# A hybrid of recurrent layers, FP4 feed-forward and attention: one root chain for both norms, the decay in PSUM, a product on GpSimd, and a new tick order

## The chip, the cores and the metric

The kernel runs on one core of a Trainium2 chip. The metric is device time in microseconds (us), the median over several executions. Of the core's engines, PE (TensorE) multiplies matrices, DVE (VectorE), ACT (ScalarE) and POOL (GpSimd) work element by element, and SP (SyncE) issues the DMAs. In this kernel all of POOL's operands lie in SBUF.

## What is computed

The input x is 16 sequences of 512 tokens with 128 channels, float32. In turn:

```
x = x + recurrent(layernorm(x))   # initial layernorm, then 4 layers
x = x + ffn(layernorm(x))         # 128 -> 352 -> 128, gated by silu, all operands through FP4 blocks of 16
x = x + attention(layernorm(x))   # causal, inner width 64
x = x + ffn(layernorm(x))         # the same weights
```

One recurrent layer is

```
h = layernorm(x); xk, xv, xr = mixes of h and h shifted by one token
k, v = xk @ Wk, xv @ Wv; sr = sigmoid(xr @ Wr)
# over tokens, with decay w and bonus u, kept in range by a running maximum pp:
out = (e1 * aa + e2 * v) / (e1 * bb + e2)     # aa, bb: decayed sums of weighted v and of weights
x = x + (sr * out) @ Wo
h = layernorm(x); x = x + sigmoid(mix_r @ Wcr) * (square(relu(mix_k @ Wck)) @ Wcv)
```

## The kernel before

All 16 sequences stay in SBUF (X, 128 partitions of tokens x 512). The work on one sequence in one layer is a job r, 64 of them (4 layers of 16); its channels x tokens tiles are 128 x 512. Each engine runs one Python loop over 133 **ticks**; in tick t the engine's order, written out by hand, calls step functions with a job number such as t - 5, and a function whose job doesn't exist does nothing. So a job goes through its steps over some 14 ticks, and many jobs are under way at once. Semaphores count finished steps; `Waits` drops waits that an engine has already passed. No planner runs: an engine executes its list in order, and a step that waits holds back what stands behind it.

Ticks 0 to 17 also normalise the input (`init_stats`, `init_rsqrt`, `init_z`, `init_affine`). `FFN_AT = NR + 3 = 67` is the base tick of 16 FFN jobs, 16 ticks later come 16 attention jobs, and 16 later 16 FFN jobs more; their steps (`mul_up`, `fh_*`, `fx_*`, `a_*`) stand in the same lists.

The steps that the text speaks of, with the tick offset of a job in the recurrent phase:
- A norm: `bn_stats` on DVE (L214), then on POOL a chain of four operations on 128 x 4 values (L590 to L595, with a pow to -1/2 at L593), each of them waiting for the one before where it uses it, then four ACT instructions (`normalise`, L734). Before, `rs1` (t - 2) and `rs2` (t - 8) run the chain once for each of the two norms of a layer.
- `turn1` transposes into PSUM bank T, `keep_h1` (ACT) takes it out; `sub_dh1` (POOL) and `mix_t`, `mix_rt` (DVE, L291, L298) mix h with its shift. `keys` (PE) writes bank K, `scan_pp` (L307) and `sub_d` read it. `args` and `exp_d` (ACT, L792 to L798) make decay and weight in the two halves of ed in SBUF; `arg_r`, `exp_r` make er.
- `mul_rv`, `mul_s1` multiply er and the weight with v (bank V, L328, L334; `mul_s1` writes back into bank V). `scan_bb` (L340) and `scan_aa` (L347) scan with the decay. `add_num` and `add_den` (POOL, L637, L631) add.
- `seeds` (ACT, L809) makes a first reciprocal rc of the denominator er, `mul_y` (DVE, L354) puts er * rc into bank K, `square_1` (ACT) squares, `mul_u`, `gated`, `scaled_p` (POOL), `rwkv` (L374) finish a cubic correction and the product with the gate; `output` (PE) and `add_xa` (L380) add to X.
- `turn2`, `keep_h2`, `sub_dh` (POOL, L650), `mix_k` (L391), `mix_r` (L398), `ff_keys` (L1090), `relu`, `square`, `ff_gate`, `tanh_c`, `ff_values` (L1107), `gate` and `add_xb` (POOL, L655) are the layer's second half.
- In the FFN jobs `fx_max`, `fh_max` take block maxima, `fx_scale` and `fh_scale` (DVE, `block_scale`, L243) the scales of 32 and 88 blocks, and POOL multiplies and divides by them (L671 to L690).

A PSUM bank has one owner at a time: `hand_over` returns the last use that a new owner must wait for. `lend_K` and `lend_O` hand a bank to a step of another engine.

## Time and profile before

| | us |
|---|---|
| median of three runs | 1459.57 (1458.12 to 1460.35) |
| the profiled execution | 1460.59 |
| its span, first to last instruction | 1459.0 |

| engine | busy us | share |
|---|---|---|
| PE | 1323.6 | 91% |
| DVE | 1344.3 | 92% |
| ACT | 1251.8 | 86% |
| POOL | 1248.4 | 86% |

The trace is of one execution. A busy share is an average over stages with different limits, so the rows below go by stretches of the span: the recurrent ticks fill it up to about 900 us, then come the first FFN, attention and the second FFN. In a timeline, times count from the span's start, and a bracket at the end of a row, where there is one, gives the idle time before it and what ended it. A duration contains what the instruction waits for inside itself.

### The profile page before, as it was taken

What the parts mean: (1) busy time and instruction counts of PE and PEld (TensorE: products, weight loads), DVE (VectorE), ACT (ScalarE), POOL (GpSimd) and SP (SyncE); (2) the same over time, 40 slices, a digit from 0 to 9 for tenths busy, and PEclk for the clock granted to TensorE, in tenths of its full rate; (3) what the DMA queues carried; (4) which work ended last, traced back from release to release, by engine and by line L of the source; (5) the groups of instructions that cost most, each with busy time, mean ns of one, the idle gap of its engine ahead of it and who ended that gap; (6) DMA issues with size and microseconds to landing.
All of it is one profiled execution on the core that took longest, in us unless ns stands there. A gap on an engine that the chain in (4) does not pass through costs nothing.

```text
span 1459.0 us, 23620 instructions
## 1 busy us (share of the span) xinstructions
PE 1323.6 (91%) x7245; PEld 936.5 (64%) x7245; DVE 1344.3 (92%) x2249; ACT 1251.8 (86%) x2459; POOL 1248.4 (86%) x1395
## 2 busy tenths in 40 slices
PE   3568899999999999999998999899999999989896
PEld 1235566666666666666666666676666788766675
DVE  6999999999999999999999999669999665799994
ACT  6679899999999999999988999778777888867764
POOL 6889999999999999999999999879998633388874
PEclk9679999999999999999999999999999999999999
DMA  7000000000000000000000000010000000000001
GB/s 222 0 1 1 1 1 1 1 1 31 2 1 1 1 1 1 1 2 1 1 1 1 1 1 8 22 30 23 23 1 2 1 1 1 1 8 24 28 22 37
DMA packets 26925, 18.56 MB, mean 13 GB/s; under 512 B 1072, under 2 KB 26160, under 8 KB 26800
## 3 DMA queue, kind: packets, MB, share of 16 engines
q1 hardware_dynamic: 26800, 17.05, 4.0%
q8 instruction: 59, 0.97, 0.3%
q14 instruction: 66, 0.54, 0.1%
HBM read 12.85 MB, written 4.19 MB: 12 GB/s over the span
## 4 chain that ended last, share of the span: by engine, by line
POOL 40%; DVE 22%; PE 18%; issue 14%; ACT 5%; POOLq 0%; DMA 0%; DVEq 0%; SPq 0%; ACTq 0%
POOL ln_rs L593 9%; POOL ln_rs L595 6%; POOL X L655 4%; POOL rv L637 4%; POOL ln_rs L590 3%; POOL dh L625 3%; POOL dh L650 3%; POOL ln_rs L591 3%; POOL er L631 3%; DVE hsc L240 3%; DVE W L450 3%; PE ps L1216 2%; PE ps L1198 2%; PE ps L1107 2%; DVE W L480 2%
## 5 line engine op out<-in xcount | busy, mean ns | idle before, releaser
L1107 PEld LDWEIGHTS ps<-W,kf 128*128 128x128 f32 x2048 | 245.2, 193 | 33.4 <-issue 28.6
L1090 PE MATMUL ps<-xk,W 128*128 128x512 f32 x512 | 255.7, 601 | 0.7 <-ACT er L874 0.7
L1107 PE MATMUL ps<-W,kf 128*128 128x128 f32 x2048 | 251.2, 276 | 1.1 <-DVE W L480 1.1
L734 ACT ACTIVATE z<-X,ln_rs 128x128 f32<-128x128 f32 x512 | 210.2, 487 | 4.7 <-POOL ln_rs L595 4.7
L593 POOL TENSOR_TENSOR ln_rs<-ln_rs,mhalf 128x4 f32<-128x4 f32 x128 | 174.0, 1360 | 0.0
L1007 PE MATMUL ps<-idn,z 128*128 128x128 f32 x664 | 105.6, 283 | 59.2 <-ACT h L828 36.7
L1007 PEld LDWEIGHTS ps<-idn,z 128*128 128x128 f32 x664 | 79.2, 144 | 122.4 <-issue 71.4
L835 ACT ACTIVATE kf<-ps 128x512 f32<-128x512 f32 x256 | 143.3, 585 | 5.5 <-PE ps L1090 5.5
L842 ACT ACTIVATE kf<-kf 128x1024 f32<-128x1024 f32 x128 | 134.3, 1049 | 0.0
L1090 PEld LDWEIGHTS ps<-xk,W 128*128 128x128 f32 x512 | 88.3, 193 | 62.1 <-issue 54.4
L1145 PE MATMUL ps<-WU,d 128*128 128x352 f32 x256 | 103.2, 485 | 20.9 <-DVE W L450 9.8
L690 POOL TENSOR_TENSOR W<-W,hsc 128x704 f32<-128x704 f32 x64 | 88.7, 1386 | 37.5 <-DVE W L480 37.5
L595 POOL TENSOR_TENSOR ln_rs<-ln_rs 128x4 f32<-128x4 f32 x128 | 107.2, 838 | 10.0
L874 ACT ACTIVATE er<-ps 128x352 f32<-128x352 f32 x128 | 58.7, 461 | 46.0 <-DVE W L450 31.5
L1138 PE MATMUL ps<-WG,d 128*128 128x352 f32 x256 | 97.5, 463 | 0.0
L214 DVE BATCH_NORM_STATS2 ln_st<-X 128x6 f32<-128x256 f32 x256 | 96.6, 418 | 0.2
L1046 PE MATMUL ps<-xt,W 128*128 128x512 f32 x128 | 73.0, 655 | 24.3 <-DVE rc L374 21.9
L1077 PEld LDWEIGHTS ps<-W,rc 128*128 128x128 f32 x512 | 71.6, 203 | 33.8 <-issue 33.8
L684 POOL TENSOR_TENSOR W<-W,hsc 128x704 f32<-128x704 f32 x64 | 88.4, 1394 | 2.9 <-DVE hsc L468 2.9
L631 POOL TENSOR_TENSOR er<-er,bb 128x512 f32<-128x512 f32 x64 | 84.9, 1326 | 4.2 <-DVE bb L340 3.5
L637 POOL TENSOR_TENSOR rv<-rv,aa 128x512 f32<-128x512 f32 x64 | 82.3, 1286 | 2.8 <-DVE aa L347 2.8
L809 ACT ACTIVATE rc<-er,seed 128x512 f32<-128x512 int32 x64 | 46.2, 722 | 44.3 <-POOL er L631 44.3
(167 smaller groups left out, 3987.9 us busy)
## 6 DMA issues: line engine op xcount, KB each, us to landing
X<-x_in SPq DMA_DIRECT2D x16, 256.0 KB, 6.8
xi<-x_in SPq DMA_DIRECT2D x16, 256.0 KB, 2.9
out<-X SPq DMA_DIRECT2D x16, 256.0 KB, 2.3
W<-weights SPq DMA_DIRECT2D x4, 832.0 KB, 8.5
W<-fp4w SPq DMA_DIRECT2D x1, 560.0 KB, 3.7
row<-rows SPq DMA_DIRECT2D x1, 192.0 KB, 3.1
wqkv<-qkv SPq DMA_DIRECT2D x1, 96.0 KB, 5.9
idn<-ident SPq DMA_DIRECT2D x1, 64.0 KB, 3.2
```

The costliest lines, as they stand in the source:

```text
L593: e.tensor_tensor(rs[:, 0, :], rs[:, 2, :], mhalf[:, :], ALU.pow).then_inc(*own.next())
L595: e.tensor_tensor(rs[:, 1, :], rs[:, 1, :], rs[:, 0, :], ALU.mult).then_inc(g.nr, 1)
L631: e.tensor_tensor(er[r % 2][:, :], er[r % 2][:, :], bb[r % 2][:, 0:T], ALU.add).then_inc(den_done, 1)
L637: e.tensor_tensor(rv[r % 2][:, :], rv[r % 2][:, :], aa[r % 2][:, 0:T], ALU.add).then_inc(num_done, 1)
L734: last = e.activation(chunk(dst, j), chunk(src, j), ACT.Identity, bias=rs[:, 1, j:j + 1], scale=rs[:, 0, j:j + 1])
L835: e.activation(kf[r % 3][:, f, :], (pF0, pF1)[f % 2][:, :], ACT.Relu).then_inc(relu_done[f], 1)
L842: e.activation(both, both, ACT.Square).then_inc(sq_done[k], 1)
L1007: last = e.transpose(chunk(dst, j), chunk(src, j), idn[:, :])
L1090: e.matmul((pF0, pF1)[f % 2][:, :], w_of(r, WCK + f), xk[r % 2][:, :], start=True, stop=True).then_inc(kf_mm[f], 1)
L1107: last = e.matmul(chunk(pKV, j), kf[r % 3][:, f, j * 128:(j + 1) * 128], w_of(r, WCV + f), start=f == 0 and j == 0, stop=f == 3, skip_grou ...
L1138: e.matmul(pG[j % 2][:, 0:I], chunk(fx[n % 2], j), WG[:, :], start=True, stop=True).then_inc(g_mm, 1)
L1145: e.matmul(pU[j % 2][:, 0:I], chunk(fx[n % 2], j), WU[:, :], start=True, stop=True).then_inc(u_mm, 1)
```

## The change

- `Norm` objects of the two norms share their buffers: one chain, `rsqrts(s)`, works on 128 x 8 values, the first norm of job s beside the second norm of job s - 6. It runs once a tick.
- `exp_d` is split. `exp_k` writes the weight in SBUF, `exp_d` writes the decay into bank T, lent by `lend_T` after `keep_h1` and taken back by `turn2` when `scan_aa` is done. `lend_K` goes.
- `mul_s1` writes weighted v to a new SBUF tile s1. Bank V is free for the next job when `mul_s1` is done.
- `mul_y` moves from DVE to POOL and multiplies in place in er; `square_1` and `rwkv` read er in SBUF.
- FFN_AT is NR + 4, so there are 134 ticks. The order of each engine's steps is new, and several steps run one tick later. The recurrent steps in their new order (offset from t; before in the printed lists):
  - DVE: `mix_t` 5, `mix_k` 10, `gated` 7, `mix_r` 11, `mul_rv` 6, `add_xa` 8, `mul_s1` 6, `scan_bb` 6, `scan_aa` 6, `bn2` 8, `scan_pp` 5, `bn1` 2, `sub_d` 5, `mul_u` 7, `gate` 13, `rwkv` 7, `mix_rt` 4, `arg_r` 5.
  - POOL: `scaled_p` 7, `mul_y` 7, `sub_dh1` 4, `add_xb` 14, `add_num` 6, `add_den` 6, `sub_dh` 9, `rsqrts` 2.
  - ACT: `exp_k` 6, `relu` 0, `exp_r` 6, `keep_h1` 4, `tanh_c` 13, `exp_d` 6, `relu` 1, `square` 1 of job 13, `norm2` 9, `relu` 2, `norm1` 3, `square_1` 7, `keep_h2` 9, `tanh_r` 6, `relu` 3, `square` 0 of job 12, `args` 5, `seeds` 6.
  - PE: `ff_keys` 0, `ff_gate` 13, `turn1` 4, `values` 6, `ff_keys` 1, `output` 8, `lend_T` 6, `ff_keys` 2, `receptance` 6, `ff_values` 0 of job 13, `keys` 5, `ff_keys` 3, `turn2` 9, `ff_values` 1.
  - FFN steps, DVE: `fh_add` 0, `fx_max`, `fh_sub` 0, `mul_up` 3, `fx_scale`, `fh_max`, `fh_add` 1, `fh_scale`, `fh_sub` 1, the two inverses, `fx_add`, `mul_up` 0, `fx_sub`, `mul_up` 1, `mul_up` 2, `f_bn`. POOL: `f_rsqrt`, `fh_scaled` 0, `add_res`, `fh_scaled` 1, `fh_divided` 0, `fx_scaled`, `fh_divided` 1, `fx_divided`.
- Two waits are new at the FFN's start: `silu` waits for the last `rwkv`, `keep_hq` for the last `scan_bb`.

```diff
@@ -29,7 +29,8 @@
 KC = [(0, 128), (128, 128), (256, 96)]
 
 Q_AT = 55
-FFN_AT = NR + 3
+FFN_AT = NR + 4
+LN2_LAG = 6
...
 
         class Norm:
-            def __init__(self, name, size):
-                self.size = size
-                self.stats, self.nr, self.z = [sem(f"{name}_{k}") for k in ("stats", "nr", "z")]
-                self.st = ring(name + "_st", size, [128, NT, 3])
-                self.rs = ring(name + "_rs", size, [128, 3, NT])
+
+            def __init__(self, name, size, lag=0, beside=None):
+                self.size, self.lag = size, lag
+                self.stats, self.z = sem(name + "_stats"), sem(name + "_z")
+                if beside:
+                    self.nr, self.st2, self.rs2, at = beside.nr, beside.st2, beside.rs2, NT
+                else:
+                    self.nr, at = sem(name + "_nr"), 0
+                    self.st2, self.rs2 = ring(name + "_st", size, [128, 2 * NT, 3]), ring(name + "_rs", size, [128, 3, 2 * NT])
+                self.st, self.rs = [k[:, at:at + NT, :] for k in self.st2], [k[:, :, at:at + NT] for k in self.rs2]
+                self.of = lambda r, n: r[(n + lag) % size]
...
-        rv, rc, ag = [ring(k, 2, [128, T]) for k in ("rv", "rc", "ag")]
+        s1, rv, rc, ag = [ring(k, 2, [128, T]) for k in ("s1", "rv", "rc", "ag")]
...
+        n_2 = Norm("ln2", 3, LN2_LAG, n_1)
...
-                w.wait_ge(g.nr, n - g.size + 1)
+                w.wait_ge(g.nr, n + g.lag - g.size + 1)
                 for k in range(NT // 2):
-                    last = e.bn_stats(g.st[n % g.size][:, 2 * k:2 * k + 2, :].rearrange("p a s -> p (a s)"),
+                    last = e.bn_stats(g.of(g.st, n)[:, 2 * k:2 * k + 2, :].rearrange("p a s -> p (a s)"),
                                       src[:, k * 256:(k + 1) * 256].rearrange("p (a c) -> p c a", a=2))
...
             def arg_r(r):
                 if 0 <= r < NR:
-                    w.wait_ge(y_done, r - 1)
+                    w.wait_ge(rwkv_done, r - 1)
                     w.wait_ge(d_done, r + 1)
...
             def mul_s1(r):
                 if 0 <= r < NR:
+                    w.wait_ge(ek_done, r + 1)
+                    w.wait_ge(v_mm, r + 1)
+                    w.wait_ge(aa_done, r - 1)
+                    e.tensor_tensor(s1[r % 2][:, :], ed[r % 2][:, 1, :], pV[:, :], ALU.mult).then_inc(s1_done, 1)
+
+            def scan_bb(r):
+                if 0 <= r < NR:
+                    w.wait_ge(den_done, r - 1)
+                    w.wait_ge(ek_done, r + 1)
                     w.wait_ge(ed_done, r + 1)
-                    w.wait_ge(rv_done, r + 1)
-                    e.tensor_tensor(pV[:, :], ed[r % 2][:, 1, :], pV[:, :], ALU.mult).then_inc(s1_done, 1)
-
-            def scan_bb(r):
-                if 0 <= r < NR:
-                    w.wait_ge(den_done, r - 1)
+                    e.tensor_tensor_scan(bb[r % 2][:, 1:T + 1], pT[:, :], ed[r % 2][:, 1, :], 0.0,
+                                         ALU.mult, ALU.add).then_inc(bb_done, 1)
+
+            def scan_aa(r):
+                if 0 <= r < NR:
+                    w.wait_ge(num_done, r - 1)
                     w.wait_ge(ed_done, r + 1)
-                    e.tensor_tensor_scan(bb[r % 2][:, 1:T + 1], ed[r % 2][:, 0, :], ed[r % 2][:, 1, :], 0.0,
-                                         ALU.mult, ALU.add).then_inc(bb_done, 1)
-
-            def scan_aa(r):
-                if 0 <= r < NR:
-                    w.wait_ge(num_done, r - 1)
                     w.wait_ge(s1_done, r + 1)
-                    e.tensor_tensor_scan(aa[r % 2][:, 1:T + 1], ed[r % 2][:, 0, :], pV[:, :], 0.0,
+                    e.tensor_tensor_scan(aa[r % 2][:, 1:T + 1], pT[:, :], s1[r % 2][:, :], 0.0,
                                          ALU.mult, ALU.add).then_inc(aa_done, 1)
-
-            def mul_y(r):
-                if 0 <= r < NR:
-                    w.wait_ge(*lent_K[r])
-                    w.wait_ge(seed_done, r + 1)
-                    e.tensor_tensor(pK[:, :], er[r % 2][:, :], rc[r % 2][:, :], ALU.mult).then_inc(y_done, 1)
...
             def rwkv(r):
                 if 0 <= r < NR:
                     w.wait_ge(u_done, r + 1)
-                    e.scalar_tensor_tensor(out=rc[r % 2][:, :], in0=pK[:, :], scalar=2.0, in1=p[r % 2][:, :],
+                    e.scalar_tensor_tensor(out=rc[r % 2][:, :], in0=er[r % 2][:, :], scalar=2.0, in1=p[r % 2][:, :],
...
-            def rsqrt(g, n, scale=1.0, eps=EPS):
-                rs, st = g.rs[n % g.size], g.st[n % g.size]
+            def roots(rs, st, done, scale=1.0, eps=EPS):
+                k = st.shape[1]
                 w.wait_ge(consts, PADS)
-                w.wait_ge(g.z, n - g.size + 1)
-                w.wait_ge(g.stats, n + 1)
                 e.tensor_scalar(rs[:, 2, :], st[:, :, 2], scale / 128.0, eps, ALU.mult, ALU.add).then_inc(*own.next())
                 e.tensor_scalar(rs[:, 1, :], st[:, :, 1], -1.0, None, ALU.mult)
                 w.wait_ge(*own.so_far())
-                e.tensor_tensor(rs[:, 0, :], rs[:, 2, :], mhalf[:, :], ALU.pow).then_inc(*own.next())
+                e.tensor_tensor(rs[:, 0, :], rs[:, 2, :], mhalf[:, 0:k], ALU.pow).then_inc(*own.next())
                 w.wait_ge(*own.so_far())
-                e.tensor_tensor(rs[:, 1, :], rs[:, 1, :], rs[:, 0, :], ALU.mult).then_inc(g.nr, 1)
+                e.tensor_tensor(rs[:, 1, :], rs[:, 1, :], rs[:, 0, :], ALU.mult).then_inc(done, 1)
+
+            def rsqrt(g, n, scale=1.0, eps=EPS):
+                w.wait_ge(g.z, n - g.size + 1)
+                w.wait_ge(g.stats, n + 1)
+                roots(g.of(g.rs, n), g.of(g.st, n), g.nr, scale, eps)
...
-            def rs1(r):
-                if 0 <= r < NR:
-                    rsqrt(n_1, r)
-
-            def rs2(r):
-                if 0 <= r < NR:
-                    rsqrt(n_2, r)
+            def rsqrts(s):
+
+                if 0 <= s < NR + LN2_LAG:
+                    lo, hi = 0 if s < NR else NT, 2 * NT if s >= LN2_LAG else NT
+                    w.wait_ge(n_1.z, min(s - 2, NR))
+                    w.wait_ge(n_2.z, s - LN2_LAG - 2)
+                    w.wait_ge(n_1.stats, min(s + 1, NR))
+                    w.wait_ge(n_2.stats, s - LN2_LAG + 1)
+                    roots(n_1.rs2[s % 3][:, :, lo:hi], n_1.st2[s % 3][:, lo:hi, :], n_1.nr)
...
+            def mul_y(r):
+                if 0 <= r < NR:
+                    w.wait_ge(seed_done, r + 1)
+                    e.tensor_tensor(er[r % 2][:, :], er[r % 2][:, :], rc[r % 2][:, :], ALU.mult).then_inc(y_done, 1)
...
             def exp_d(r):
                 if 0 <= r < NR:
+                    w.wait_ge(*lent_T[r])
                     w.wait_ge(args_done, r + 1)
-                    e.activation(ed[r % 2][:, :, :], ed[r % 2][:, :, :], ACT.Exp, scale=-1.0).then_inc(ed_done, 1)
+                    e.activation(pT[:, :], ed[r % 2][:, 0, :], ACT.Exp, scale=-1.0).then_inc(ed_done, 1)
+
+            def exp_k(r):
+                if 0 <= r < NR:
+                    w.wait_ge(args_done, r + 1)
+                    e.activation(ed[r % 2][:, 1, :], ed[r % 2][:, 1, :], ACT.Exp, scale=-1.0).then_inc(ek_done, 1)
...
-                    e.activation(pO[:, :], pK[:, :], ACT.Square, bias=seed[:, 1:2]).then_inc(sq1_done, 1)
+                    e.activation(pO[:, :], er[r % 2][:, :], ACT.Square, bias=seed[:, 1:2]).then_inc(sq1_done, 1)
...
             def values(r):
                 if 0 <= r < NR:
-                    w.wait_ge(*bV.hand_over(aa_done, r + 1))
+                    w.wait_ge(*bV.hand_over(s1_done, r + 1))
...
-            def lend_K(r):
-
-                if 0 <= r < NR:
-                    lent_K[r] = bK.hand_over(rwkv_done, r + 1)
+            def lend_T(r):
+
+                if 0 <= r < NR:
+                    lent_T[r] = bT.hand_over(aa_done, r + 1)
```

## Rows read from the trace of the kernel before

**Rows 1.** Windows: start:end length, busy (count) of PE, PEld, DVE, ACT, POOL, clock, DMA.

```profile
208.60:691.60 483.00, 466.29 (x2522) 322.25 (x2521) 483.00 (x736) 461.47 (x841) 466.07 (x491) 1.00 0.01 3
889.60:1009.20 119.60, 113.44 (x637) 83.20 (x636) 93.26 (x158) 97.70 (x187) 103.77 (x113) 0.97 0.08 23
1009.20:1072.20 63.00, 59.95 (x340) 42.72 (x339) 63.00 (x109) 50.56 (x103) 61.55 (x67) 1.00 0.06 18
1175.60:1229.80 54.20, 54.20 (x366) 43.98 (x365) 33.30 (x105) 46.09 (x134) 20.27 (x35) 1.00 0.00 1
1309.80:1397.90 88.10, 79.67 (x454) 57.97 (x453) 88.10 (x143) 67.14 (x137) 72.10 (x78) 1.00 0.09 25
```

**Rows 2.** DVE timeline: start us, duration us, engine, line, operation, out<-in.

```profile
499.51 0.66 DVE L380 TENSOR_TENSOR X<-X,ps 128x512 f32<-128x512 f32 x1
...
501.37 1.42 DVE L398 SCALAR_TENSOR_TENSOR xc<-dh,vec,h 128x512 f32<-128x512 f32 x1
...
503.37 0.69 DVE L354 TENSOR_TENSOR ps<-er,rc 128x512 f32<-128x512 f32 x1
...
505.04 0.74 DVE L391 SCALAR_TENSOR_TENSOR xk<-dh,vec,h 128x512 f32<-128x512 f32 x1
505.70 1.21 DVE L340 TENSOR_TENSOR_SCAN bb<-ed 128x512 f32<-128x512 f32 x1
...
507.42 0.68 DVE L360 SCALAR_TENSOR_TENSOR p<-ps,p 128x512 f32<-128x512 f32 x1
...
513.31 0.65 DVE L380 TENSOR_TENSOR X<-X,ps 128x512 f32<-128x512 f32 x1
```

**Rows 3.** POOL timeline of the same tick.

```profile
500.97 1.27 POOL L637 TENSOR_TENSOR rv<-rv,aa 128x512 f32<-128x512 f32 x1
...
505.23 1.67 POOL L595 TENSOR_TENSOR ln_rs<-ln_rs 128x4 f32<-128x4 f32 x1
506.99 0.56 POOL L590 TENSOR_SCALAR ln_rs<-ln_st 128x4 f32<-128x4 f32 x1
...
507.82 1.04 POOL L593 TENSOR_TENSOR ln_rs<-ln_rs,mhalf 128x4 f32<-128x4 f32 x1
...
509.09 1.27 POOL L631 TENSOR_TENSOR er<-er,bb 128x512 f32<-128x512 f32 x1
510.32 1.03 POOL L650 TENSOR_TENSOR dh<-h 128x512 f32<-128x512 f32 x1
```

**Rows 4.** FFN: POOL timeline; then L243's instructions, ns min/median/max.

```profile
1050.88 0.19 POOL L590 TENSOR_SCALAR ff_rs<-ff_st 128x4 f32<-128x4 f32 x1
...
1052.62 1.39 POOL L690 TENSOR_TENSOR W<-W,hsc 128x704 f32<-128x704 f32 x1
...
L243 DVE TENSOR_SCALAR xsc<-xsc x32: 160/492/1234, 936.1 to 1404.3; 128x32 f32<-128x32 f32 x32
L243 DVE TENSOR_SCALAR hsc<-hsc x32: 195/522/1393, 973.7 to 1438.6; 128x88 f32<-128x88 f32 x32
```

**Rows 5.** Waits, 208.6 to 691.6 us, ACT and PE: total, times, longest.

```profile
ACT rc L809 <- POOL er L631: 21.5, 35, 0.6
...
PE ps L1007 <- ACT h L828: 16.7, 35, 0.5
```

**Rows 6.** Groups by line: count, busy us, mean ns, idle before.

```profile
L798 ACT ACTIVATE ed<-ed 128x1024 f32<-128x1024 f32 x64 | 68.0, 1063 | 0.0
...
L803 ACT ACTIVATE er<-er 128x512 f32<-128x512 f32 x64 | 40.8, 638 | 1.4 <-DVE er L321 1.4
```

**Rows 7.** PE timeline of a recurrent tick.

```profile
507.77 1.88 PE L1090 MATMUL ps<-xk,W 128*128 128x512 f32 x4
509.49 1.02 PE L1046 MATMUL ps<-xt,W 128*128 128x512 f32 x2
...
512.96 1.95 PE L1107 MATMUL ps<-W,kf 128*128 128x128 f32 x16
```

**Rows 8.** Line 307's instructions: ns min/median/max, first and last start.

```profile
L307 DVE TENSOR_TENSOR_SCAN pp<-wneg,ps x64: 1182/1193/1244, 26.4 to 902.3; 128x512 f32<-128x512 f32 x64
```

More of the change, by code:

```diff
@@ L519, in vector @@
             for t in range(TICKS):
-                fh_max(ffn_job(t - 7))
+                mix_t(t - 5)
+                fh_add(ffn_job(t - 8), 0)
+                fx_max(ffn_job(t - 3))
+                a_mask(att_job(t - 7), 3)
+                fh_sub(ffn_job(t - 8), 0)
+                init_affine(t - 2)
+                mul_up(ffn_job(t - 7), 3)
+                fx_scale(ffn_job(t - 3))
+                fh_max(ffn_job(t - 7))
+                weights_rounded(t - Q_AT - 6)
+                mix_k(t - 10)
@@ L521, in vector @@
+                gated(t - 7)
+                mix_r(t - 11)
+                mul_rv(t - 6)
+                a_max(att_job(t - 7), 3)
+                add_xa(t - 8)
+                mul_s1(t - 6)
+                scan_bb(t - 6)
+                prepare(t - 3)
                 fh_add(ffn_job(t - 8), 1)
+                scan_aa(t - 6)
                 fh_scale(ffn_job(t - 7))
+                a_inverse(att_job(t - 8))
                 fh_sub(ffn_job(t - 8), 1)
-                mul_up(ffn_job(t - 6), 0)
@@ L525, in vector @@
[L525 to L533 removed]
+                fx_inverse(ffn_job(t - 3))
+                fh_inverse(ffn_job(t - 7))
+                a_add(att_job(t - 8))
+                bn2(t - 8)
@@ L543, in vector @@
-                a_max(att_job(t - 6), 1)
-                mul_y(t - 7)
-                mix_t(t - 4)
-                arg_r(t - 5)
-                a_mask(att_job(t - 6), 2)
-                a_max(att_job(t - 6), 2)
-                mix_k(t - 10)
-                init_affine(t - 1)
-                scan_bb(t - 6)
-                gated(t - 6)
-                weights_scales(t - Q_AT)
-                mul_u(t - 7)
-                mul_rv(t - 5)
-                rwkv(t - 7)
-                gate(t - 12)
@@ L954, in scalar @@
             for t in range(TICKS):
+                keep_hq(ffn_job(t - 9), 0)
+                silu(ffn_job(t - 7), 3)
+                put_x(ffn_job(t - 9))
+                keep_hq(ffn_job(t - 9), 2)
+                exp_k(t - 6)
+                keep_hq(ffn_job(t - 9), 1)
+                relu(t - 11, 0)
+                exp_r(t - 6)
+                keep_h1(t - 4)
+                tanh_c(t - 13)
+                fh_magic(ffn_job(t - 8), 1)
+                exp_d(t - 6)
+                relu(t - 11, 1)
@@ new lines, in tensor @@
+                ff_gate(t - 13)
+                turn1(t - 4)
+                values(t - 6)
+                lend_M(ffn_job(t - 8), 1)
+                ff_keys(t - 11, 1)
+                output(t - 8)
+                lend_T(t - 6)
+                f_turn(ffn_job(t - 5))
+                ff_keys(t - 11, 2)
+                f_gate(ffn_job(t - 6), 0)
+                p_values(att_job(t - 8))
+                receptance(t - 6)
+                down(ffn_job(t - 9))
+                f_up(ffn_job(t - 6), 0)
@@ new lines, in tensor @@
+                p_turn(att_job(t - 7), 0)
+                lend_X(ffn_job(t - 4))
+                f_gate(ffn_job(t - 6), 1)
+                f_up(ffn_job(t - 6), 1)
+                ff_values(t - 13, 0)
+                similarity(att_job(t - 6), 0)
+                p_turn(att_job(t - 7), 1)
+                keys(t - 5)
+                f_gate(ffn_job(t - 6), 2)
+                lend_O(t - 7)
+                similarity(att_job(t - 6), 1)
+                ff_keys(t - 11, 3)
+                turn2(t - 9)
```

204 lines of the change are left out of this document (79 added, 125 removed).

## The prediction

> **What bounds the kernel now.** The busy shares of the whole span are close together on four engines, so no share alone names the bound. The table by stretch [rows 1] gives four stages. From 208.6 to 691.6 us (35 recurrent ticks) the span per tick is 483.0/35 = 13.80 us; DVE is busy all of it, PE 96.5%, ACT 95.5%, POOL 96.5%. From 1009.2 to 1072.2 (6 ticks of the first FFN) a tick is 10.5 us, with DVE full and POOL 61.55 of 63. From 1309.8 to 1397.9 (8 ticks of the second) it is 11.0, DVE full, POOL only 72.1 of 88.1. From 1175.6 to 1229.8 (7 ticks of attention) it is 7.74, and PE is busy 54.2 of 54.2: PE bound, and the change takes nothing off PE.
>
> The DVE's timeline of one recurrent tick [rows 2] shows what "full" means. `add_xa` returns after 513.31 - 499.51 = 13.80. An instruction starts about 0.08 before its predecessor's recorded end (505.04 + 0.74 against 505.70), so an operation's place is its duration less 0.08. `mix_r` takes 1.42 where `mix_k`, the same form, takes 0.74: 0.68 is a wait inside the instruction. So DVE's own work is 13.12 a tick. POOL's timeline [rows 3] shows for what. GpSimd is in `add_num` until 502.24 when `mix_r` starts at 501.37; and POOL's first chain of tiny operations (L590 to L595) takes until 506.99, so 4.75 us, the second 509.09 - 506.99 = 2.10. The same chain in the FFN takes 1052.62 - 1050.88 = 1.74 [rows 4]. The slow stretch is exactly where DVE runs operations with two SBUF inputs or in a double-rate form, back to back from `mix_r` (501.37) to `mul_u` (507.42): 6.05 us, 5.37 without the wait. L595 starts at 505.23 and ends at 506.90, when `scan_bb` (505.70 + 1.21) ends. These DVE operations and POOL's exclude each other.
>
> That gives a sum for POOL. Big operations: four at 1.23 (510.32 - 509.09) and two at 0.99 (1.03 less the same 0.04) are 6.90. Two chains less their pow of 1.04, which mostly runs while DVE holds its inputs, are 2 x (1.74 - 1.04) = 1.40. DVE's excluding stretch is 5.37. Together 13.67, against 13.80 measured; 0.13 is loss at the seams. **So DVE and POOL together bound the tick.** ACT has 0.61 idle a tick (21.5/35, behind the denominator on POOL) and PE 0.48 (16.7/35, behind h2) [rows 5]: ACT has 13.19 of work, PE 13.32 with its pipeline drain, about 13.15 without.
>
> Were the exclusion strict for the pow too, the tick before would be 6.90 + 2 x 1.74 + 5.37 = 15.75; the trace has 13.80, so the pow is not held out for its whole length.
>
> The Trainium skill ("SBUF — State Buffer", section "Who interferes with whom") calls this an exclusive lock between a DVE operation with two SBUF inputs and a GpSimd one that reads SBUF: the later one blocks until the other ends. It speaks against moving one more SBUF operation to GpSimd, and taken at its word for the pow as well it gives the second rival's time, where the trace only half agrees.
>
> **The change, part by part (recurrent tick).**
> - `mul_y` leaves DVE: -0.61 (0.69 less 0.08) there, and +1.23 on POOL, priced by `add_den` [rows 2, 3].
> - One chain for both norms: POOL loses a chain of 1.74. The pow gets eight columns for four. No row has one of eight: it costs between 1.04 (all fixed) and 2.08 (all per column). I take 2.08, since the chain's three other operations share 0.70 with their gaps, which leaves most of a pow looking like work per column; but it hides under DVE's excluding stretch either way.
> - Decay in PSUM: `scan_bb` now has one SBUF input and leaves the excluding stretch (-1.13 there, no change on DVE's own time; between 0 and 0.05 for reading PSUM, I take 0). `rwkv` now reads er and p from SBUF and enters it (+0.66, the place of `mix_k`; +0.06 on DVE). Weighted v in SBUF: at nothing, its inputs are one SBUF and one PSUM as before; bank V comes free earlier.
> - The double-width exp (L798, 1.063) becomes two of 512 columns (L803, 0.638 each) [rows 6]. Less one start overlap of 0.11 that is +0.11 on ACT. `square_1` reads SBUF: this exp, SBUF to SBUF, is the nearest row, and a price between 0 and 0.05 is left; I take 0.
> - New order: `rwkv`, `mix_rt`, `arg_r`, `mix_t`, `mix_k`, `gated`, `mix_r` follow each other round the tick's end. The excluding stretch is 5.37 - 0.61 - 1.13 + 0.66 = 4.29, and POOL's chain is issued last in its tick, opposite it.
>
> New sums. DVE: 13.12 - 0.61 + 0.06 = 12.57. POOL with the stretch: 6.90 + 1.23 + 0.70 + 4.29 = 13.12, plus the same seam loss 13.25. ACT: 13.30. PE: 13.15 to 13.32. Four limits within 0.75, so the tick can't fall to DVE's 12.57. Do the waits fit? On PE a 512-column product takes 2 x 0.43 = 0.86 (four instructions in 509.49 - 507.77 = 1.72) and one half of the FFN values 1.8, so 0.9 for eight and 0.45 for four small products [rows 7]. In the new order, from `ff_keys` 0 on, `turn1` is done at 0.86 + 0.9 + 0.45 = 2.2, and `turn2` starts at 2.2 + 1.72 (values) + 0.86 + 0.9 + 0.86 + 0.86 + 1.8 + 0.86 + 0.86 = 10.9. Keys of the recurrent part are done at 10.0, so DVE's `scan_pp` starts there, and by DVE's order (0.68 for `bn2`, 1.13 for each scan) `scan_aa` ends at 9.4: bank T's new loan to the decay keeps about 1.4 of slack; if it didn't, `turn2` would wait with the second half of the FFN values behind it on PE, and `keep_h2` behind that on ACT. On DVE `scan_bb` now waits for the separate decay exp, with `scan_aa`, `bn2` and `scan_pp` behind it; the exp follows `turn1` (2.2), h1, and a tanh, so it ends by about 6, and the scan is due at 7.1. Estimates from the same rows: the denominator's product on POOL is done near 8, almost 3 before ACT squares it; dh2 has its h2 only 0.4 before POOL's turn. I take **13.40**: the largest sum plus 0.1 for the tight places; -0.40 a tick. Bounds are 13.25 and 13.80.
>
> From tick 13 to 66 there are 54 filled ticks (the scans of 64 jobs start from 26.4, in tick 4, to 902.3, in tick 67 [rows 8]): 54 x 0.40 = -21.6. In the first 13 ticks and the 4 that also normalise the input, DVE or POOL limits with nothing else near, and up to 1.2 a tick (0.61 and the 0.68 wait) can be had; bounds 0 and -12, I take -5.
>
> **One tick more.** FFN_AT goes from NR+3 to NR+4: 134 ticks for 133. Work isn't added, only idle. From 889.6 to 1009.2 (11 ticks of draining and filling, 10.9 each) PE is busy 113.4 of 119.6, so between 0 and 10.9, and I take the 6.2 us by which PE is idle in such a stretch: +6.
>
> **FFN stages.** DVE's work there is unchanged. Its two block scales (L243) find GpSimd busy: 195 ns and 160 ns at least, 522 and 492 in the median, up to 1393 and 1234 [rows 4]. In the first FFN POOL itself is full at 10.5, so no gain. In the second 11.0 less DVE's own 9.85 (the 10.5 of the first less waits of 0.33 + 0.33) leaves 1.15. In the new order `fh_scale` stands where POOL waits for the halves of h, so I expect half of that back in some 10 ticks: -5; bounds -11 and +16. Attention: 0. New waits (silu behind `rwkv`, keep_hq behind `scan_bb`) end ticks before they are asked: nothing. DMAs aren't moved (the queue on SP has its order and waits as before).
>
> Sum: -21.6 - 5 + 6 - 5 = -25.6. The profiled run took 1460.59 (span 1459.0 and 1.6 around it), 1.0 over the median of the runs, 1459.57. So 1460.6 - 25.6 - 1.0 = 1434.
>
> The Trainium skill ("VectorE: DVE Perf Modes", section "The TRN2 errata — SBUF-src ops pay a fixed extra latency per instruction") gives ScalarE 52 cycles at 1.2 GHz more for an SBUF source: 0.04 us for `square_1`, an estimate of 3 us over 64 ticks; no run here shows it yet.
>
> **Rivals.**
> 1. The tick stays near 13.7, because POOL's tight place fails: the wide pow and the late dh2 push the chain past the excluding stretch, `mul_y` is then fully paid and DVE waits for POOL again. For it: POOL has gained a 1.23 operation and its sum is as high as any. Against: DVE may now lose 0.8 a tick unseen. -0.1 x 54 - 2 + 6 - 2 = -3: **1456**.
> 2. A strict exclusion, the pow held out for its whole length: 6.90 + 1.23 + (1.74 + 1.04) + 4.29 = 15.2, that is +1.4 a tick: 1460 + 76 + 6 = 1542. The 13.80 of before, where it would have given 15.75, speaks against it. Chance 0.02.
> 3. Slower, by the block scales in both FFN stages. In the new order `fx_scale` follows `mul_up` 3 and `fh_scale` follows the second `fh_add`. If each lands at the start of a POOL block multiply (L690, 1.39), DVE has 9.85 + 2 x 1.2 = 12.3 a tick, +1.8 in 10 ticks and +1.3 in 10: +31. With -20.6 of the rest: 1459.6 + 10 = **1470**. It decides from 1 us a tick more in those 20 ticks. Speaks for it: maxima of 1.39 exist. Against: POOL idles where `fh_scale` now stands.
> 4. The change works better than I dare: tick 13.25, extra tick free, FFN2 at its 9.85: -30 - 8 - 11 = **1411**.
>
> **Chances.** Forecast (1422 to 1447) 0.60; rival 1 (1447 to 1462) 0.18; rival 3 0.10; rival 4 (below 1422) 0.10; rival 2 0.02. The range takes the forecast's own and most of rivals 1 and 4: 1416 to 1457. About 0.2% (2.9 us) is what a measurement of this kernel can tell from no change: of rival 1 a quarter lies within it, so faster 0.83, same 0.05, slower 0.12.
>
> **What would show it.** Recurrent tick 13.3 to 13.5 between two `scan_pp`; DVE then no longer full (94%), PE and ACT at 99%; `mix_r` at 0.74; POOL's one chain under 4.7 us; pow 1.04 to 2.1; second FFN's tick below 11.0; attention at 7.7. Wrong if any mix waits for POOL over 0.7 us, if ACT waits for `mul_y`, or if the FFN ticks pass 11.5.

## The result: 1414 us for 1460, and the profile after

The changed kernel takes 1414.21 us in the median of 4 runs (1412.23 to 1419.29), the one before 1459.72: a ratio of 0.9695, 95% interval 0.9669 to 0.9722. The forecast was 1434, with a range down to 1416. So the direction was right and the gain, 45 us, was almost twice what was forecast; the time lies below the range. The profiled execution took 1414.5, with a span of 1413.1.

Where the 45.9 us between the two spans went can be read from two instructions of the trace: `scan_pp` of the first and of the last recurrent job, and the FFN's `fh_max` of its first and last. First the changed kernel (ns min/median/max, then first and last start in us):

```profile
L315 DVE TENSOR_TENSOR_SCAN pp<-wneg,ps x64: 1161/1222/1228, 25.3 to 865.0; 128x512 f32<-128x512 f32 x64
...
L248 DVE TENSOR_REDUCE hsc<-W x32: 1605/1620/1621, 936.6 to 1391.1; 128x88 f32<-128x1408 f32 x32
```

The second one in the kernel before (its scans are [rows 8]):

```profile
L240 DVE TENSOR_REDUCE hsc<-W x32: 1560/1601/1609, 972.1 to 1436.2; 128x88 f32<-128x1408 f32 x32
```

| stretch | before | after | difference |
|---|---|---|---|
| start to the first scan | 26.4 | 25.3 | -1.1 |
| first to last scan | 875.9 | 839.7 | -36.2 |
| last scan to first fh_max | 69.8 | 71.6 | +1.8 |
| first to last fh_max | 464.1 | 454.5 | -9.6 |
| last fh_max to the end | 22.8 | 22.0 | -0.8 |

The first row is no effect of the change: the kernels of the experiments below, most of them this one with a small edit, have their first scan at 26.0 to 26.5.

Of the 36.2, the first 13 intervals between scans give 5.2 and the other 50 give 31.0. The stretches of the changed kernel that answer to [rows 1] are these (the same columns; two windows of the recurrent phase, then the first FFN, attention, the second FFN):

```profile
202.30:293.50 91.20, 91.20 (x504) 64.41 (x503) 89.40 (x141) 91.20 (x174) 85.62 (x79) 1.00 0.00 1
293.50:676.20 382.70, 382.70 (x2089) 265.10 (x2088) 374.93 (x580) 382.70 (x727) 348.72 (x320) 1.00 0.01 4
...
972.60:1035.50 62.90, 58.06 (x337) 43.28 (x337) 62.87 (x109) 49.17 (x103) 61.53 (x66) 1.00 0.06 18
1133.80:1187.60 53.80, 53.80 (x367) 43.88 (x367) 33.88 (x106) 45.83 (x136) 21.44 (x39) 1.00 0.01 1
1281.10:1332.20 51.10, 48.03 (x280) 36.00 (x280) 51.10 (x91) 40.77 (x86) 45.19 (x50) 1.00 0.09 27
```

The 29 recurrent ticks of the second window take 382.7/29 = 13.20 each. PE and ACT are busy in all of it, DVE in 98%, POOL in 91%: the bound has gone over from DVE and POOL to ACT and PE. The page's chain of the work that ended last shows the move too, first before, then after:

```profile
POOL 40%; DVE 22%; PE 18%; issue 14%; ACT 5%; POOLq 0%; DMA 0%; DVEq 0%; SPq 0%; ACTq 0%
...
PE 63%; DVE 24%; issue 7%; ACT 3%; POOL 2%; DMA 0%; DVEq 0%; SPq 0%; ACTq 0%; POOLq 0%
```

The chain gives ACT only 3%, although ACT is as full as PE in the recurrent ticks. Which of the two binds there is settled by the runs that take work off each of them, further down.

The first FFN's tick is 62.9/6 = 10.5, as before; attention's 53.8/7 = 7.69 for 7.74; the second FFN's 51.1/5 = 10.2 for 11.0.

DVE's timeline of a recurrent tick (start us, duration us; beside [rows 2]):

```profile
504.65 1.22 DVE L315 TENSOR_TENSOR_SCAN pp<-wneg,ps 128x512 f32<-128x512 f32 x1 [0.17 <-PE ps L1068]
...
508.41 0.91 DVE L379 SCALAR_TENSOR_TENSOR rc<-er,p 128x512 f32<-128x512 f32 x1
509.25 0.74 DVE L306 SCALAR_TENSOR_TENSOR sr<-dh,vec,h 128x512 f32<-128x512 f32 x1
...
512.23 0.75 DVE L403 SCALAR_TENSOR_TENSOR xc<-dh,vec,h 128x512 f32<-128x512 f32 x1
512.89 0.68 DVE L336 TENSOR_TENSOR rv<-er,ps 128x512 f32<-128x512 f32 x1
...
517.84 1.22 DVE L315 TENSOR_TENSOR_SCAN pp<-wneg,ps 128x512 f32<-128x512 f32 x1 [0.17 <-PE ps L1068]
```

`mix_r` (L403) is at 0.75, so it no longer waits, and the excluding stretch runs from `rwkv` (508.41) to `mul_rv` (512.89), 4.48 us. `rwkv`'s 0.91 holds a wait of 0.2 for POOL, whose `sub_dh` runs until 508.78. POOL beside it (beside [rows 3]):

```profile
507.74 1.04 POOL L664 TENSOR_TENSOR dh<-h 128x512 f32<-128x512 f32 x1 [0.92 <-ACT h L848]
508.86 0.52 POOL L592 TENSOR_SCALAR ln_rs<-ln_st 128x8 f32<-128x8 f32 x1
...
510.06 1.85 POOL L595 TENSOR_TENSOR ln_rs<-ln_rs,mhalf 128x8 f32<-128x8 f32 x1
511.99 0.39 POOL L597 TENSOR_TENSOR ln_rs<-ln_rs 128x8 f32<-128x8 f32 x1
512.39 1.72 POOL L657 TENSOR_TENSOR p<-p,rc 128x512 f32<-128x512 f32 x1
514.08 1.27 POOL L651 TENSOR_TENSOR er<-er,rc 128x512 f32<-128x512 f32 x1
```

The joint chain takes 512.39 - 508.86 = 3.5 us, wholly against DVE's stretch, and POOL sits idle for 0.92 a tick before `sub_dh` (L664), which makes the second norm's dh from the h that ACT delivers. `scaled_p` (L657) starts at 512.39 and ends at 514.11, which is 1.2 after `mix_r` ended at about 512.9; unhindered it is recorded with 1.27. By the Trainium skill ("SBUF — State Buffer", section "Who interferes with whom") the later of the two blocks until the other has ended, and this row agrees within 0.1.

### The profile page after: what moved, and what is told of

It reads as the page before. It is cut to its first block, busy times and chain, and to the rows that moved or that the text cites. A ratio compares the mean times of both kernels' runs of the same rounds, so it can differ in the third digit from the quotient of the medians.

```text
span 1413.1 us, 23624 instructions
## 1 busy us (share of the span) xinstructions
PE 1305.1 (92%) x7245; PEld 931.7 (66%) x7245; DVE 1280.8 (91%) x2185; ACT 1253.0 (89%) x2525; POOL 1179.1 (83%) x1227
## 4 chain that ended last, share of the span: by engine, by line
PE 63%; DVE 24%; issue 7%; ACT 3%; POOL 2%; DMA 0%; DVEq 0%; SPq 0%; ACTq 0%; POOLq 0%
PE ps L1129 14%; PE ps L1112 13%; PE ps L1029 4%; PE ps L1119 4%; PE ps L1099 3%; PE ps L1082 3%; PE ps L1068 3%; PE ps L1075 3%; PE ps L1076 3%; DVE hsc L248 3%; PE ps L1238 2%; PE ps L1167 2%; PE ps L1220 2%; DVE W L455 2%; DVE W L485 2%
## 5 line engine op out<-in xcount | busy, mean ns | idle before, releaser
L1112 PE MATMUL ps<-xk,W 128*128 128x512 f32 x512 | 266.3, 603 | 1.4 <-DVE W L455 1.4
L748 ACT ACTIVATE z<-X,ln_rs 128x128 f32<-128x128 f32 x512 | 233.0, 667 | 4.3 <-POOL ln_rs L597 4.3
L855 ACT ACTIVATE kf<-ps 128x512 f32<-128x512 f32 x256 | 195.9, 765 | 3.1 <-PE ps L1112 3.1
L862 ACT ACTIVATE kf<-kf 128x1024 f32<-128x1024 f32 x128 | 158.1, 1235 | 0.0
L595 POOL TENSOR_TENSOR ln_rs<-ln_rs,mhalf 128x8 f32<-128x8 f32 (+1 forms) x70 | 124.5, 1779 | 0.0
L657 POOL TENSOR_TENSOR p<-p,rc 128x512 f32<-128x512 f32 x64 | 105.2, 1644 | 12.1 <-DVE p L373 7.8
L664 POOL TENSOR_TENSOR dh<-h 128x512 f32<-128x512 f32 x64 | 66.8, 1044 | 36.4 <-ACT h L848 36.3
L1119 PEld LDWEIGHTS ps<-W,xc 128*128 128x128 f32 x512 | 68.0, 194 | 35.9 <-ACT sr L798 17.5
L315 DVE TENSOR_TENSOR_SCAN pp<-wneg,ps 128x512 f32<-128x512 f32 x64 | 77.8, 1216 | 8.2 <-PE ps L1068 8.2
L651 POOL TENSOR_TENSOR er<-er,rc 128x512 f32<-128x512 f32 x64 | 81.5, 1273 | 0.0
```

The costliest lines, as they stand in the source:

```text
L595: e.tensor_tensor(rs[:, 0, :], rs[:, 2, :], mhalf[:, 0:k], ALU.pow).then_inc(*own.next())
L657: e.tensor_tensor(p[r % 2][:, :], p[r % 2][:, :], rc[r % 2][:, :], ALU.mult).then_inc(ps_done, 1)
L748: last = e.activation(chunk(dst, j), chunk(src, j), ACT.Identity, bias=rs[:, 1, j:j + 1], scale=rs[:, 0, j:j + 1])
L855: e.activation(kf[r % 3][:, f, :], (pF0, pF1)[f % 2][:, :], ACT.Relu).then_inc(relu_done[f], 1)
L862: e.activation(both, both, ACT.Square).then_inc(sq_done[k], 1)
L1112: e.matmul((pF0, pF1)[f % 2][:, :], w_of(r, WCK + f), xk[r % 2][:, :], start=True, stop=True).then_inc(kf_mm[f], 1)
```

## The experiments

The theory: POOL's loop through its large operations, its chains and DVE's excluding stretch was the bound, and the joint chain takes it out of the way; ACT and PE are next. Ticks are the intervals between two `scan_pp` in the steady part. The first rival is that the new order made the gain, the second that work taken off DVE did. Ratios are to the kernel before on the same chip, with 95% intervals. A part "of the first 13 intervals" is one of those in which the input is still being normalised, "the other 50" is the rest.

### The chain taken apart again

```diff
...
-                    roots(n_1.rs2[s % 3][:, :, lo:hi], n_1.st2[s % 3][:, lo:hi, :], n_1.nr)
+                    for at in range(lo, hi, NT):
+                        rs, st = n_1.rs2[s % 3][:, :, at:at + NT], n_1.st2[s % 3][:, at:at + NT, :]
+                        roots(rs, st, n_1.nr if at + NT == hi else None)
```

> The changed kernel with the root chain taken apart again: two chains of four operations on 128 x 4, one behind the other, in the place of the joint one. Theory of the sum (POOL's big operations + its chains less their pow + DVE's excluding stretch + 0.13 bounds the tick as soon as it passes PE and ACT): 8.13 + 1.40 + 4.29 + 0.13 = 13.95 a recurrent tick for 13.19, some 55 ticks, +41 us: about 1455. Theory of the order (the new order made the gain, single costs on POOL are hidden): at most +5, about 1418.

Measured: 1456.8 us, ratio 0.9977 (0.9967 to 0.9988), a tick of 13.77. Nearly the whole gain is gone, with everything else of the change in place. POOL's timeline:

```profile
509.68 0.57 POOL L592 TENSOR_SCALAR ln_rs<-ln_st 128x4 f32<-128x4 f32 x1
...
511.80 1.27 POOL L659 TENSOR_TENSOR p<-p,rc 128x512 f32<-128x512 f32 x1
...
518.95 1.48 POOL L666 TENSOR_TENSOR dh<-h 128x512 f32<-128x512 f32 x1
520.51 0.52 POOL L592 TENSOR_SCALAR ln_rs<-ln_st 128x4 f32<-128x4 f32 x1
...
523.45 0.57 POOL L592 TENSOR_SCALAR ln_rs<-ln_st 128x4 f32<-128x4 f32 x1
```

From 520.51 one chain runs to 523.45 against DVE's stretch, the other takes 2.12 (509.68 to 511.80, and again from 523.45) behind it; there is no idle time left on POOL. The order's theory is out for the recurrent phase. The sum's time came within 2 us, but by luck: its tick of 13.95 is 0.18 too long, and that is made up by 8.7 us in the first 13 intervals, which it had not singled out.

### The product back on DVE

```diff
 (DVE's list)
                 mix_r(t - 11)
+                mul_y(t - 7)
```

with the function moved as it is, writing er in SBUF.

> The changed kernel with the product of denominator and seed back on DVE, in SBUF, right behind mix_r. Theory of the sum: POOL 6.90 + 0.70 + (4.29 + 0.66) + 0.13 = 12.68, DVE 12.57 + 0.66 = 13.23, ACT 13.19: tick 13.25, +3 us: about 1417. Rival (taking work off DVE is what made the kernel faster): a tick near 13.8, +34: about 1448.

Measured: 1428.3 us, ratio 0.9786 (0.9769 to 0.9804). The steady tick is 13.19, as in the changed kernel: there the move to GpSimd is worth nothing. But 14 us are lost, which neither theory had:

```profile
L315 DVE TENSOR_TENSOR_SCAN pp<-wneg,ps x64: 1162/1200/1223, 26.4 to 879.5; 128x512 f32<-128x512 f32 x64
```

First to last scan is 853.1 for 839.7. 8.8 of these 13.4 fall into the first 13 intervals, where DVE has the input's statistics and affine step besides and is busy 99% of the time. Five of the first eight intervals are 0.6 longer, which is `mul_y` counted in full; two others are shorter, and the eight together give 2.1. The last five give 6.6, and what makes them is not shown: from 147 to 212 us this run had a mean clock of 0.92 of the full 2.4 GHz, with stretches at 1.2 GHz, where the changed kernel had 1.00 from 144 to 202. The other 4.6 lie among the irregular ticks of the later 50.

### The decay back in SBUF

```diff
-                    e.activation(pT[:, :], ed[r % 2][:, 0, :], ACT.Exp, scale=-1.0).then_inc(ed_done, 1)
+                    e.activation(ed[r % 2][:, 0, :], ed[r % 2][:, 0, :], ACT.Exp, scale=-1.0).then_inc(ed_done, 1)
```

with both scans reading it there, and `args` waiting for `scan_aa`.

> The changed kernel with the decay in SBUF again (bank T still handed round as before), so that scan_bb has two SBUF inputs; nothing else moved. Theory of the sum: DVE's excluding time grows by 1.13, 13.12 + 1.13 + 0.13 = 14.38 a tick, +65 us: about 1479. Rival (the scan stands opposite POOL's large operations and DVE has 0.6 us a tick to spare, so only the rest is paid): tick 13.5 or less, +17: about 1431.

Measured: 1486.8 us, ratio 1.0182 (1.0163 to 1.0201), a tick of 14.08: slower than before the change. DVE:

```profile
512.57 1.74 DVE L350 TENSOR_TENSOR_SCAN bb<-ed 128x512 f32<-128x512 f32 x1
514.23 1.99 DVE L358 TENSOR_TENSOR_SCAN aa<-ed,s 128x512 f32<-128x512 f32 x1
```

and POOL at the same time:

```profile
513.18 1.95 POOL L634 TENSOR_TENSOR dh<-h 128x512 f32<-128x512 f32 x1
515.09 2.18 POOL L669 TENSOR_TENSOR X<-X,cr 128x512 f32<-128x512 f32 x1
```

Both scans now have two SBUF inputs (decay and s1 as well as decay and weight), so both wait and are waited for: 0.53 and 0.79 on DVE over their 1.21 and 1.20, 0.9 each on POOL over 1.03 and 1.27. The theory had counted one scan only, and its time is near the measured one by luck: it forecast a tick of 14.38, and with both scans its sum would be 13.12 + 2 x 1.13 + 0.13 = 15.5, where 14.08 was measured; 17.8 of the 70.3 us of longer span came in the first 13 intervals. So decay in PSUM and weighted v in SBUF are a pair: together they leave each scan one SBUF input. The run undoes one half of the pair and so gives `scan_aa` two SBUF inputs, which it didn't have before; it doesn't say what the pair is worth against the kernel before.

### The joint chain alone, in the kernel before

The old order, old buffers, `mul_y` on DVE, 133 ticks; only the two norms' roots are joined:

```diff
-                rs1(t - 2)
+                rsqrts(t - 2)
                 weights_scaled(t - Q_AT - 13)
-                rs2(t - 8)
```

> The kernel before, in its own order, with the joint root chain alone. Theory of the sum: POOL 13.67 - 0.70 = 12.97, so DVE's own 13.12 bounds, tick 13.2, -33 us: about 1427. Theory of the order (an order not drawn up for it can't use it; norm2 gets its roots at another place): at most -0.2 a tick, 1449 or more.

Measured: 1426.3 us, ratio 0.9764 (0.9748 to 0.9781). This one edit brings 34 of the 45 us. The tick is 13.10, less than the changed kernel's 13.20, in which ACT has the split exp. DVE, with no wait left in `mix_r`:

```profile
510.21 0.74 DVE L406 SCALAR_TENSOR_TENSOR xc<-dh,vec,h 128x512 f32<-128x512 f32 x1
...
523.32 0.74 DVE L406 SCALAR_TENSOR_TENSOR xc<-dh,vec,h 128x512 f32<-128x512 f32 x1
```

POOL:

```profile
510.49 0.53 POOL L596 TENSOR_SCALAR ln_rs<-ln_st 128x8 f32<-128x8 f32 x1 [1.11 <-DVE ln_st L222]
511.10 1.23 POOL L597 TENSOR_SCALAR ln_rs<-ln_st 128x8 f32<-128x8 f32 x1
512.29 2.12 POOL L599 TENSOR_TENSOR ln_rs<-ln_rs,mhalf 128x8 f32<-128x8 f32 x1
```

POOL now waits 1.11 a tick for DVE's statistics where it used to be without a gap. PE, DVE and ACT are all busy from 300 to 640 us without a gap. By their own work, DVE has the prediction's 13.12, ACT 13.07 (worked out below) and PE the 13.10 at which the run with less on ACT stands, so this run can't tell which of the three makes the tick.

### The move of the product alone, in the kernel before

```diff
 (DVE's list)
-                mul_y(t - 7)
 (POOL's list)
                 scaled_p(t - 6)
+                mul_y(t - 6)
```

er gets a third buffer, `square_1` and `rwkv` read it there.

> The kernel before, in its own order and with its two chains, with the product of denominator and seed alone moved to POOL (in place in er, behind scaled_p; er gets a third buffer, which the old order needs; square_1 and rwkv read er). Theory of POOL's loop (big operations plus the two chains as they run against DVE's excluding stretch): 6.90 + 1.23 + 6.85 = 15.0 a tick for 13.80, 55 ticks, +65 us: about 1525. Rival (offloading DVE pays by itself, POOL has room): 13.2 a tick, -33: about 1427.

Measured: 1502.6 us, ratio 1.0295 (1.0281 to 1.0309), a tick of 14.43. The sign and the mechanism hold, the size doesn't: 43 us for 65. With `mul_y` off DVE the excluding stretch is shorter and the two chains run faster through it: 6.85 was their time against the old stretch, here it is 3.4 and 2.3, and `add_num` is 0.5 longer before them, since it meets `mix_r`. POOL's two chains and the `add_den` behind them:

```profile
512.01 0.52 POOL L583 TENSOR_SCALAR ln_rs<-ln_st 128x4 f32<-128x4 f32 x1
...
515.41 0.56 POOL L583 TENSOR_SCALAR ln_rs<-ln_st 128x4 f32<-128x4 f32 x1
...
517.73 1.27 POOL L624 TENSOR_TENSOR er<-er,bb 128x512 f32<-128x512 f32 x1
```

### Less on ACT, less on PE, less on both

```diff
-                    both = kf[r % 3][:, 2 * k:2 * k + 2, :]
+                    both = kf[r % 3][:, 2 * k:2 * k + 2 - k, :]
```

> The changed kernel with 0.43 us a tick less on ACT: the second square of a recurrent job covers 512 columns and leaves the other 512 unsquared. Theory (in the steady ticks of 13.19 ACT binds, with PE's 13.10 right below): a tick of 13.10, some 40 ticks, -4 us: about 1410. Rival (PE binds alone): no change, 1414.

Measured: 1412.0 us, ratio 0.9676 (0.9661 to 0.9690); the steady tick is 13.10, and ACT now waits 0.3 a tick for PE, which has no gap.

```diff
 (ff_gate)
-                    for j in range(NT):
+                    for j in range(1):
```

> The changed kernel with some 0.67 us a tick less on PE: the gate's product of the second half is made for one token block of four (the other three blocks keep what the bank held). Theory (ACT binds): the steady tick stays 13.19, the few ticks of 13.10 come up to it, -1 to 0: 1413 to 1414. Rival (PE binds): 12.5 to 12.8 a tick, -25: about 1390.

Measured: 1410.9 us, ratio 0.9669 (0.9655 to 0.9684); the steady tick is 13.20, and PE now waits 0.5 a tick for ACT, which has no gap. Both times are below the changed kernel's by no more than their intervals, so it is the ticks and the waits that decide, and they are those of the theory: ACT binds at 13.20, PE follows at 13.10. (The 3 us of the second time below its forecast lie in the drain before the first `fh_max`, 68.3 for 71.6.)

> Both cuts in one kernel: 0.43 us of squares and 0.67 us of gate products left out a tick. Theory A (POOL's loop is its big operations and the longer of DVE's excluding stretch and the chain that runs against it, 8.13 + 4.29 = 12.4, since POOL sits idle 0.9 a tick in the changed kernel): ACT with 12.76 and DVE with 12.7 bind, tick 12.8, -20 us: about 1394. Theory B (the sum of the prediction holds, 13.25 with the seams, and POOL stands right behind ACT): no change beyond the 13.10 of some ticks, 1410 or more.

Measured: 1391.2 us, ratio 0.9538 (0.9522 to 0.9554), a tick of 12.77. Theory A's time was 1394. The stretch from 400 to 640 us:

```profile
400.00:640.00 240.00, 238.68 (x1245) 159.43 (x1244) 238.21 (x377) 240.00 (x473) 229.81 (x207) 1.00 0.00 1
```

ACT alone is wholly full, and the tick is its 13.20 less the 0.43 left out, though PE and DVE are within 1% of full. So the 13.25 of the prediction for POOL, the sum with 0.13 for seams, was not a limit of the changed kernel; its loop is at most 12.8.

### One tick more

```diff
-FFN_AT = NR + 4
+FFN_AT = NR + 5
```

> The changed kernel with FFN_AT one tick later again (NR + 5, 135 ticks), so that one tick more lies between the recurrent phase and the FFN. Theory (the change's own extra tick was free only because it fell into the start, where x and the constants are still landing; in the drain a tick costs the idle it adds): +6 to +9 us, about 1421. Rival (an extra tick costs nothing anywhere, since the work is the same): 1414.

Measured: 1419.1 us, ratio 0.9723 (0.9709 to 0.9738); its interval touches the changed kernel's. By the two marks, its span is 3.7 longer, 1.2 at the start, where this edit does nothing, and 2.7 between the last scan and the first `fh_max`. That would be some 3 us of the 10.9 that a tick takes, less than the theory's 6. But the same stretch takes 67.5 to 73.2 in the other runs above and below that leave `FFN_AT` as the changed kernel has it, so the 2.7 isn't clear of what other edits do there.

### Two instructions moved in the old order

From the kernel before with the joint chain:

```diff
-                fh_scale(ffn_job(t - 7))
                 fh_sub(ffn_job(t - 8), 1)
+                fh_scale(ffn_job(t - 7))
...
-                fx_scale(ffn_job(t - 3))
...
+                fx_scale(ffn_job(t - 3))
                 fx_inverse(ffn_job(t - 3))
```

> The kernel before with the joint chain (1426 us) and two more edits in its old DVE order: fh_scale moved behind the second fh_sub, fx_scale moved right ahead of fx_inverse, both to where POOL stands between two operations. Theory (in the second FFN DVE binds and these two wait for GpSimd inside the instruction, 0.74 and 0.39 a tick): its tick falls from 11.0 to 9.9, the first FFN's stays 10.5 (POOL is full), -11 us: about 1415. Rival (the FFN tick hangs on a chain through ACT and PE, the waits only fill it): 10.8 or more, -2: about 1424.

Measured: 1415.6 us, ratio 0.9701 (0.9687 to 0.9714); the second FFN's tick is 10.24, for 11.02 and the 9.9 expected. That is the changed kernel's time within what can be measured, with one chain and two moved lines, and without its PSUM decay, its product on GpSimd or its new order. DVE in the second FFN:

```profile
1333.82 0.17 DVE L251 TENSOR_SCALAR xsc<-xsc 128x32 f32<-128x32 f32 x1
...
1338.28 0.20 DVE L251 TENSOR_SCALAR hsc<-hsc 128x88 f32<-128x88 f32 x1
```

and POOL:

```profile
1333.89 0.20 POOL L596 TENSOR_SCALAR ff_rs<-ff_st 128x4 f32<-128x4 f32 x1
...
1338.44 1.39 POOL L703 TENSOR_TENSOR W<-W,hsc 128x704 f32<-128x704 f32 x1 [0.42 <-DVE W L488]
```

Each scale slips in just ahead of a POOL operation and is at its least; with the joint chain alone they took 0.57 and 0.95 in these ticks. The tick falls 0.36 less than these waits; what takes the rest up is not shown.

The first FFN didn't stay as expected. Its steady tick rose from 10.52 to 10.82, with `fx_scale` at 0.75 there for 0.50 before the move, while `fh_scale` fell from 0.53 to 0.20. Its last six intervals, in which attention's jobs come in, fell by 3.0 together. So a place that is free in one stage isn't in another.

### A version meant to beat both

The changed kernel with `fh_scale` behind the second `fh_sub`, and then with 128 columns of one relu made by DVE:

```diff
-                fh_scale(ffn_job(t - 7))
                 a_inverse(att_job(t - 8))
                 fh_sub(ffn_job(t - 8), 1)
+                fh_scale(ffn_job(t - 7))
```

> The changed kernel with fh_scale moved behind the second fh_sub, where POOL has just finished an operation. Theory: its 0.55 becomes 0.2, the second FFN's tick 10.25 becomes 9.9, -3.5 us: about 1410.5. Rival (POOL's next block multiply starts at the same moment and fh_scale waits as long or longer): 1414 or more.

Measured: 1414.0 us, ratio 0.9684 (0.9670 to 0.9697); the second FFN's tick is 10.04 for 10.25. `fh_scale` is at its 0.20 there, and first to last `fh_max` is 3.7 us shorter, as the theory had it, but the time doesn't resolve it.

```diff
...
+                    w.wait_ge(relu_done[1], r + 1)
+                    e.tensor_scalar(kf[r % 3][:, 1, 384:T], pF1[:, 384:T], 0.0, None, ALU.max).then_inc(relu_v, 1)
...
-                    e.activation(kf[r % 3][:, f, :], (pF0, pF1)[f % 2][:, :], ACT.Relu).then_inc(relu_done[f], 1)
+                    n = 384 if f == 1 else T
+                    e.activation(kf[r % 3][:, f, 0:n], (pF0, pF1)[f % 2][:, 0:n], ACT.Relu).then_inc(relu_done[f], 1)
```

The square, the last `ff_keys` and the FFN's second bank get a wait for DVE's piece.

> The last kernel with 0.11 us a recurrent tick taken off ACT besides: DVE makes the last 128 of 512 columns of the second relu. Theory (ACT binds at 13.19, PE at 13.10 next, DVE has 0.5 to spare): 13.10 a tick, -3.5 us more: about 1407. Rival (the new wait of PE and ACT for DVE's piece costs more than the 0.09): 1411 or more.

Measured: 1411.9 us, ratio 0.9676 (0.9663 to 0.9689), the steady tick 13.10 as expected, but the time is the rival's and not the 1407 of the theory: 3.2 us came off the later 50 intervals and 1.5 were lost in the first 13. It is 2.4 us below the changed kernel, and the intervals overlap: not clearly better.

## Why the prediction was right in the bound and wrong in the size

The spans differ by 45.9 where the sum had 25.6, so 20.3 are missing. By its own terms:

- **The bound and the mechanism** were right. DVE and POOL bound the old tick together: one chain less in the kernel before brings 13.80 down to 13.10, one chain more in the changed kernel brings 13.20 up to 13.77. **What failed is three terms of the sum**, all taken too cautiously: the tick, the extra tick and the FFN stages.
- **The tick: 13.40 forecast, 13.20 measured** (-31.0 us in the 50 later intervals for the -21.6 of 54 ticks; 9.4 of the 20.3). Two terms of it were mis-sized. ACT's work was taken as 13.80 less an idle time of 0.61 [rows 5]. That idle time counts from the recorded end of the instruction before. In the kernel before:

```profile
509.06 0.79 ACT L778 ACTIVATE h<-ps,vec 128x512 f32<-128x512 f32 x1
510.45 0.72 ACT L809 ACTIVATE rc<-er,seed 128x512 f32<-128x512 int32 x1 [0.61 <-POOL er L631]
```

`keep_h1` would have let its successor start after 0.66, not 0.79 (506.47 to 507.13 below for its like in the second norm). So ACT was free for 0.73 and its work was 13.07; the times from start to start of its other instructions add up to the same. With 0.11 for the split exp (0.52 and 0.54 from start to start for 0.95) and some 0.05 for `square_1`, it is the 13.2 that binds, where the prediction had 13.30. The text subtracted the overlap on DVE and POOL and not here. The other term, 0.1 for tight places, had no row and was not needed: the waits left in the steady tick are on POOL (0.92, and 0.5 in `scaled_p`) and on DVE (0.2 in `rwkv`, 0.17 before `scan_pp`), none on ACT or PE. And the POOL sum of 13.25 had its seam loss carried over; the run with less on ACT and PE shows at most 12.8.
- **The extra tick: +6 forecast, +1.8 measured in the drain** (4.2 of the 20.3; another 1.1 is the start of the profiled run, which no edit explains). The step that failed was to take the whole of PE's idle time in the drain as the price of a tick. A further tick comes to 2.7 there, and other edits move that stretch as much, so its price is a few us at most and not better known.
- **The FFN stages: -5 forecast, -10.4 measured** (5.4 of the 20.3). The mechanism was right. In the second FFN the halving was the error: `fx_scale` came down to 0.17 and `fh_scale` to 0.55, 0.75 a tick of the 1.15, and its 15 intervals fell by 6.7 together. The first FFN, put at no gain, gave 4.1 in its 15 intervals, 3.0 of it in the last six, where attention's jobs come in. The old order with only the two scales moved gives the same 3.0 in these six, so the place of the scales is enough for it. The gap to the second FFN grew by 1.2 and the end fell by 0.8.
- **The first ticks: -5 forecast, -5.2 measured.** This is where the product's move can have paid, since its undoing costs 8.8 here, some of that perhaps by the clock; in steady ticks it is free to undo.
- **Rival 1** (the chain spills past the stretch) didn't come about: 3.5 us of chain in 4.48. The pow of eight columns takes 1.85 there, close to the 2.08 taken. **Rival 2**, the strict exclusion with the pow held out, is out: the pow's 1.85 lies wholly inside DVE's stretch. The pairs of large operations in the rows above, in both kernels and in the run with the decay in SBUF, do wait for each other to the end. **Rival 3** was decided by where the scales met POOL, and they met it mostly at gaps. **Rival 4**, at 1411 the nearest to the truth, was given 0.10. Its 30 for the tick was right (31.0). Its 11 for the FFN was right by luck, since 4.1 of the 10.4 came from the first FFN, where it had none, and its 8 for the first ticks were 5.2. The forecast had taken a cautious value for each term and so was cautious three times over, and the low end of its range cut rival 4 off.
